# A decoder layer on one core: other phases for the stages of the feed-forward and cross-attention part, and x rounded two rows at a time

## The reference

```python
x = _layernorm(x + _L0_attn_ref(x, ...))        # gated linear attention, 16 heads
x = _layernorm(x + _L0_xattn_ref(x, ctx, Wq, bq, Wk, bk))
x = _layernorm(x + _L0_ffn_ref(x, w_gate, w_up, w_down))

def _L0_xattn_ref(x, ctx, Wq, bq, Wk, bk):
    query, key = ctx @ Wq.T + bq, ctx @ Wk.T + bk           # 512 x 128 each
    return x @ softmax(query @ key.T)                       # over the feature axis of x

def _L0_ffn_ref(x, w_gate, w_up, w_down):                   # 2048 inner features
    gate, up = bitlinear(x, w_gate), bitlinear(x, w_up)
    return bitlinear(fwht(silu(gate) * up), w_down)

def bitlinear(x, w):       # per token: round(x * 128/absmax) in -128..127; w ternary
    return act_quant(x) @ weight_quant(w).T
```

## Time and profile before

| | |
|---|---|
| median of 3 runs | 1765.03 us (1763.45 to 1766.21) |
| the profiled execution | 1764.3 us, of which the span of the instructions is 1762.5 |
| granted TensorE clock, mean | 0.958 |
| busy: TensorE, VectorE, ScalarE, GpSimd | 1569.6, 1050.5, 678.7, 468.5 us |
| first gate, end of the span | 1264.4, 1762.5 us |

### The profile page before, as it was taken

How to read it: one execution, slowest core, us unless ns; L and a number is a source line. 1 busy time by engine, 2 the same in 40 slices (tenths; PEclk the granted TensorE clock), 3 DMA queues, 4 the chain that set the end, 5 groups by cost and what they waited for, 6 DMA issues and landing times. The chain is left out here.

```text
span 1762.5 us, 24103 instructions
## 1 busy us (share of the span) xinstructions
PE 1569.6 (89%) x9570; PEld 1233.5 (70%) x9570; DVE 1050.5 (60%) x1962; ACT 678.7 (39%) x1276; POOL 468.5 (27%) x334
## 2 busy tenths in 40 slices
PE   7999999999999999999999999987676868878765
PEld 5888777888788887888877878875453545655553
DVE  4555655556555566565565655667666667765544
ACT  4323323223233233332332323322356566576632
POOL 1112001012001113333443333310255543344300
PEclk9999999999999999999999999998888989999887
DMA  7011101101111001211111111021011332323430
GB/s 252 31 49 37 49 30 53 32 31 59 38 36 55 25 13 48 67 36 61 60 44 65 54 50 57 27 94 74 13 42 56 100 96 66 92 76 108 127 106 18
DMA packets 86527, 107.00 MB, mean 61 GB/s; under 512 B 4496, under 2 KB 58896, under 8 KB 86032
## 3 DMA queue, kind: packets, MB, share of 16 engines
q1 hardware_dynamic: 84496, 99.17, 17.5%
q0 software_dynamic: 1920, 6.29, 0.9%
HBM read 78.19 MB, written 27.26 MB: 60 GB/s over the span
## 5 line engine op out<-in xcount | busy, mean ns | idle before, releaser
L350 PE MATMUL bank<-Wh,XTh 128*128 128x512 f32 x512 | 211.5, 413 | 0.0
L352 PE MATMUL bank<-Wh,XTl 128*128 128x512 f32 x512 | 200.8, 392 | 0.0
L351 PE MATMUL bank<-Wl,XTh 128*128 128x512 f32 x512 | 199.9, 390 | 0.0
L682 ACT ACTIVATE V<-bank 128x256 f32<-128x256 f32 x128 | 49.1, 384 | 373.2 <-PE bank L352 373.1
L1257 POOL TENSOR_TENSOR sm<-sm,half 128x8 f32<-128x8 f32 x32 | 52.8, 1649 | 522.9 <-DVE sm L973 522.9
L350 PE MATMUL bank<-XTh,Wh 128*128 128x512 f32 x384 | 160.9, 419 | 12.1 <-DVE XTl L868 12.1
L352 PE MATMUL bank<-XTh,Wl 128*128 128x512 f32 x384 | 151.0, 393 | 0.0
L351 PE MATMUL bank<-XTl,Wh 128*128 128x512 f32 x384 | 150.2, 391 | 0.0
L908 DVE SCALAR_TENSOR_TENSOR U<-U,bank 128x256 f32<-128x256 f32 x128 | 53.6, 419 | 148.3 <-ACT U L684 148.3
L563 PE MATMUL bank<-XT,W 128*128 128x512 bf16 x512 | 125.8, 390 | 11.9 <-ACT H L808 7.0
L1292 POOL TENSOR_TENSOR M<-GS,M 128x512 f32<-128x512 f32 x64 | 81.9, 1280 | 182.3 <-ACT GS L796 168.8
(11 more groups left out here) (188 smaller groups left out, 3423.9 us busy)
## 6 DMA issues: line engine op xcount, KB each, us to landing
z_scratch<-EV SPq DMA_DIRECT2D x64, 256.0 KB, 2.0
Z<-z_scratch SPq DMA_DIRECT2D x16, 1024.0 KB, 5.8
RAW<-wgT SPq DMA_DIRECT2D x16, 512.0 KB, 3.8
RAW<-wuT SPq DMA_DIRECT2D x16, 512.0 KB, 3.7
RAW<-wdT SPq DMA_DIRECT2D x16, 512.0 KB, 3.7
w_scratch<-BW POOLq DMA_DIRECT2D x24, 256.0 KB, 4.3
W<-w_scratch SPq DMA_DIRECT2D x3, 2048.0 KB, 14.0
RAW<-Wo SPq DMA_DIRECT2D x8, 512.0 KB, 3.8
```

Source lines behind the costliest of these rows:

```text
L350: engine.matmul(o, lh(c), rh(c), start=c == 0, stop=False)
L351: engine.matmul(o, lh(c), rl(c), start=False, stop=False)
L352: last = engine.matmul(o, ll(c), rh(c), start=False, stop=c == n - 1)
L682: engine.activation(V[:, par, i, :], bk[:, 0:256], ACT.Copy).then_inc(S["v_evac"], 1)
```

## The change

In the feed-forward list, `clamp` of tile i goes from step 4i+27 to 4i+29, `turn_q` from 4i+28 to 4i+31, `down` from 4i+29 to 4i+32 and `store` from 4i+30 to 4i+33; `quantise` stays at 4i+26. The list is three steps longer. The cross stages get a table of their own places (`BESIDE`): `qk` goes from the last step of a block into the first one of the next, behind its gate; the four normalisations of n1 become a stage; `x101` and `x123` join `energy23` and `att_scale`; `x_turned` goes from the 14th to the 16th step of a block. In the seam `n1` stands behind `energy23`, and `leave_o` ahead of `xm3`. `x_round` is now two stages of two rows each, with the small scale operations twice, for two rows each time.

```diff
+CROSS = ("ctx", "qk", "n1", "energy01", "energy23", "att_scale", "att01", "att23", "x101", "x123", "xm0", "xm1",
+         "xm2", "xm3", "x_round0", "x_round1", "x_made", "x_turned")
+
+BESIDE = {0: ("qk",), 1: ("n1",), 2: ("energy01",), 3: ("energy23", "x101"), 4: ("att_scale", "x123"),
+          5: ("att01",), 6: ("att23",), 8: ("xm0",), 9: ("xm1",), 10: ("xm2",), 11: ("xm3", "x_round0"), 12: ("x_round1",),
+          13: ("x_made",), 15: ("x_turned",)}
...
-        if n % 4 == 3 and 0 <= (n - 27) // 4 < 16:
-            yield "clamp", (n - 27) // 4
+        if n % 4 == 1 and 0 <= (n - 29) // 4 < 16:
+            yield "clamp", (n - 29) // 4
...
-        if n < 46:
-            yield CROSS[(n + 2) % 16], (n + 2) // 16 + 1
-        if n % 4 == 0 and 0 <= (n - 28) // 4 < 16:
-            yield "turn_q", (n - 28) // 4
-        if n % 4 == 1 and 0 <= (n - 29) // 4 < 16:
-            yield "down", (n - 29) // 4
+        if b < 3:
+            for stage in BESIDE.get(j, ()):
+                yield stage, b + 1
+        if b < 2 and j == 14:
+            yield "ctx", b + 2
+        if n % 4 == 3 and 0 <= (n - 31) // 4 < 16:
+            yield "turn_q", (n - 31) // 4
+        if n % 4 == 0 and 0 <= (n - 32) // 4 < 16:
+            yield "down", (n - 32) // 4
...
-                elif stage == "x_round":
-                    act.wait_ge(S["x_scale"], b + 1)
+                elif stage in ("x_round0", "x_round1"):
+                    k = int(stage[7])
+                    act.wait_ge(S["x_scale"], 2 * b + k + 1)
...
-                    for i in range(4):
+                    for i in (2 * k, 2 * k + 1):
...
+                elif stage == "n1":
+                    for i in range(4):
+                        normalise("n1", 4 * b + i, i)
```

More of the change, by code:

```diff
@@ L74, in seam_order @@
     return (("keys", last), ("ctx", 0), ("scores", last), ("states", last), ("turn_o", last - 1), ("qk", 0),
-            ("ok", last), ("y", last - 1), ("turn_ok", last), ("energy01", 0), ("energy23", 0), ("turn_w", last), ("att01", 0),
+            ("ok", last), ("y", last - 1), ("turn_ok", last), ("energy01", 0), ("energy23", 0), ("n1", 0), ("turn_w", last), ("att01", 0),
             ("weights", last), ("att23", 0), ("x101", 0), ("x123", 0), ("values", last), ("xm0", 0), ("xm1", 0),
-            ("turn_o", last), ("xm2", 0), ("xm3", 0), ("leave_o", 0), ("x_round", 0), ("y", last), ("leave_y", 0),
+            ("turn_o", last), ("xm2", 0), ("leave_o", 0), ("xm3", 0), ("x_round0", 0),
+            ("x_round1", 0), ("y", last), ("leave_y", 0),
             ("x_made", 0), ("x_turned", 0))
-CROSS = ("ctx", "qk", "energy01", "energy23", "att_scale", "att01", "att23", "x101", "x123", "xm0", "xm1", "xm2",
-         "xm3", "x_round", "x_made", "x_turned")
+CROSS = ("ctx", "qk", "n1", "energy01", "energy23", "att_scale", "att01", "att23", "x101", "x123", "xm0", "xm1",
[3 more added lines that the diff above has]
+          13: ("x_made",), 15: ("x_turned",)}
 def ffn_order():
-    yield CROSS[0], 1
-    yield CROSS[1], 1
-    for n in range(64 + 27):
+    yield "ctx", 1
+    for n in range(64 + 30):
+        b, j = divmod(n, 16)
         if 0 <= n - 22 < 64:
@@ L98, in ffn_order @@
             yield "read", (n - 18) // 4
-        if n % 4 == 3 and 0 <= (n - 27) // 4 < 16:
-            yield "clamp", (n - 27) // 4
+        if n % 4 == 1 and 0 <= (n - 29) // 4 < 16:
+            yield "clamp", (n - 29) // 4
         if n % 4 == 2 and 0 <= (n - 26) // 4 < 16:
             yield "quantise", (n - 26) // 4
-        if n < 46:
-            yield CROSS[(n + 2) % 16], (n + 2) // 16 + 1
-        if n % 4 == 0 and 0 <= (n - 28) // 4 < 16:
-            yield "turn_q", (n - 28) // 4
-        if n % 4 == 1 and 0 <= (n - 29) // 4 < 16:
-            yield "down", (n - 29) // 4
-        if n % 4 == 2 and 0 <= (n - 30) // 4 < 16:
-            yield "store", (n - 30) // 4
+        if b < 3:
[7 more added lines that the diff above has]
+            yield "down", (n - 32) // 4
+        if n % 4 == 1 and 0 <= (n - 33) // 4 < 16:
+            yield "store", (n - 33) // 4
 def raw_tasks():
@@ L547, in cross @@
                     bk = take(("spread", b), (S["s_evac"], b + 1))
-                    pe.wait_ge(S["x_scaled"], b + 1)
+                    pe.wait_ge(S["x_scaled"], 4 * b + 4)
                     for i in range(4):
@@ L1053, in cross @@
                     row_max(b, 1)
-                    normalise("n1", 4 * b, 0)
-                    normalise("n1", 4 * b + 1, 1)
                 elif stage == "energy23":
@@ L1094, in cross @@
                     dve.wait_ge(S["y_mm"], 4 * STEPS)
[L1095 to L1098, removed]
+                elif stage in ("x_round0", "x_round1"):
+                    k = int(stage[7])
+                    q = ax[:, b, :, 2 * k:2 * k + 2]
+                    if k:
+                        finish(b, 3)
+                    dve.wait_ge(S["x_absmax"], 4 * b + 2 * k + 2)
                     engine.tensor_scalar(q[:, 0, :], q[:, 0, :], EPS, 1.0 / 128, ALU.max,
                                          ALU.mult).then_inc(S["x_limit"], 1)
-                    dve.wait_ge(S["x_limit"], b + 1)
+                    dve.wait_ge(S["x_limit"], 2 * b + k + 1)
                     engine.reciprocal(q[:, 1, :], q[:, 0, :]).then_inc(S["x_scale"], 1)
@@ L1106, in cross @@
                     engine.tensor_scalar(q[:, 3, :], q[:, 0, :], ws[:, 1, 0:1], float(1.0 / np.sqrt(np.float32(FF))),
-                                         ALU.mult, ALU.mult)
+                                         ALU.mult, ALU.mult).then_inc(S["x_scaled"], 1)
                 elif stage == "x_made":
@@ L1140, in ffn_tile @@
                     dve.wait_ge(S["h_scale"], 4 * i + 1)
+                    dve.wait_ge(S["x_scaled"], 4 * b + 4)
                     engine.tensor_scalar(f[:, 6:7], f[:, 4:5], ax[:, b, 3, i % 4:i % 4 + 1], EPS, ALU.mult,
```

## The result

The changed kernel takes 1772.01 us (median of 5 runs, 1771.09 to 1772.50); the kernel before took 1763.45 us beside it (5 runs, 1762.53 to 1766.21). The ratio is 1.0044, 95% interval 1.0029 to 1.0059: slower, by 8.6 us between the medians, where 1756 was forecast. The profiled execution took 1771.41 us, its span is 1769.6, 7.1 more than before.

A forecast was written before the change was run, and what follows sets the result against it. The prediction took a ScalarE-VectorE ring to pace the feed-forward steps, with TensorE's wait for the clamp mostly lead. Its terms, -13.7-1.3+4.5-2.8+5.0 = -8.3 us on 1764.3, gave 1756; own range 1748 to 1763, with rivals 1739 to 1773.

The forecast's parts named there:

- the sum: Whole kernel: -13.7-1.3+4.5-2.8+5.0 = -8.3 us on the profiled 1764.3, giving 1756.0.
- Start and block 0: Feed-forward start to tanh 16: gate 0 and tanh 0 fit under the first wait, tanh 16 at 1344.8, -13.7 us.
- Block 1: Tanh 16 to tanh 32: steps sum to 102.0 us against 103.3 before, -1.3.
- Block 2: Tanh 32 to tanh 48: stages paired otherwise, the merged step dear; 116.2 us against 111.7 before, +4.5.
- Block 3: Tanh 48 to tanh 63, without cross stages: 80.9 us, -2.8.
- the ring: Feed-forward steps: ScalarE and VectorE alternate, each starting when the other ends, 4.48 us from eviction to eviction in a late step.
- The wait for the clamp: TensorE's 42.4 us ahead of turn_q: mostly lead over ScalarE and VectorE, so it goes with blocks 2 and 3 hardly shorter.
- The rival that TensorE's waits pace the kernel: Feed-forward part: removing TensorE's waits gains about 37 us, 1728, or 1742 with the tail alone TensorE-bound; chance 0.15.
- The tail: Tanh 63 to the end: 14.1 us per tile against 15.1, but one tile more behind the last gate; 110.3 us, +5.0.
- its sign of being wrong: The forecast would be wrong if block 2 fell below 105 us or the tail's interval left 13.5 to 15.
- the rival: Behind the last gate: each down at the lower clock, 6.2 us, interval 16.4, tail 125.1, total 1771; chance 0.25.

The follow-up runs named there:

- cross part alone: The change with the feed-forward tile stages (clamp, turn_q, down, store) back at their old places: 1753.19 us, ratio 0.9929.
- tile part alone: The kernel before with only clamp, turn_q, down and store at the places of the change: 1784.13 us, ratio 1.0104.
- long filler: The change with 22 useless matmuls into an unread bank ahead of each down from tile 8 on: 1761.62 us, ratio 0.9992.
- short filler: The change with eight useless matmuls into an unread bank ahead of each down from tile 8 on: 1770.86 us, ratio 1.0029.
- late `down`: The change's cross-attention places with clamp and turn_q at old places, down and store two steps later than in the kernel before: 1711.62 us, ratio 0.9707.

## Why the prediction was wrong

The sign was wrong by one term, the duration of `down` behind the last gate. The profiled execution is 15.4 us above the sum: 10.6 are the tail's, 4.8 the blocks'. Without the tail's the change would have been 3.5 us faster. By the prediction's own steps:

**Start and block 0: right, and 3.3 us too modest.** Gate 0 and tanh 0 went into the wait for the low half (tanh 0 at 1256.83). Tanh 1 was put at 1269.6 and came at 1266.2, because `qk` did not take the 5.3 us of the earlier trace rows:

```profile
1258.19 0.50 PE L358 MATMUL bank<-X1h,XH 128*128 128x512 f32 x1 [2.12 <-POOL X1l L1275]
...
1260.83 0.39 PE L360 MATMUL bank<-X1h,XL 128*128 128x512 f32 x1
1261.06 1.25 PE L571 MATMUL bank<-XT,W 128*128 128x512 bf16 x5
```

TensorE idles 2.12 us instead of 5.83 ahead of it, since gate 0 is its filler, and it does `qk` in 3.0 us: the clock over `qk` is 1.00, and was 0.50 before. The forecast had kept the slow clock for `qk` although it had put work in front of it: the error of the tail with the other sign. From tanh 1 to 16 were 75.3 us, forecast 75.2.

**Block 1: right.** 100.7 against 102.0.

**Block 2: the sign right, the size too small.** 120.1 against 116.2. The cross part alone has 116.4 there, the tile part alone 113.7, before 111.7: +4.7 and +2.0, and some 1.7 more together. The cross part is the dear one, as forecast. By steps the miss sits in 43 to 45, with `x_round0`, `x_round1` and `x_made`: put at 19.7 together, they took 23.9, and 22.3 in the cross part alone. The slow `down` in step 44 (5.20 us) is not it: with the long filler that `down` took 3.61 and the step 7.8 all the same. The step with the four normalisations was put at 7.3 and took 7.4; here they are, and below them those of block 0:

```profile
1452.96 3.85 DVE L1018 TENSOR_SCALAR Y<-Y,mv,rs 128x512 f32<-128x512 f32 x4
```

```profile
1266.05 1.91 DVE L1018 TENSOR_SCALAR Y<-Y,mv,rs 128x512 f32<-128x512 f32 x4
```

In block 0 GpSimd does nothing from 1265.36 to 1267.63, nearly to their end, and the four take 1.91 us (block 1 the same); in block 2 GpSimd's product begins at 1453.34, among them, and they take 3.85. The Trainium skill, "SBUF — State Buffer", section "SBUF: two separate sides", states that a VectorE operation in a two-port mode and a GpSimd one each hold the pair of ports which they share for the whole instruction. The trace agrees. The forecast had 2.0 for the four without a collision and 3.3 with one.

**Block 3: the sign wrong.** 86.4 against 80.9. In the timeline of TensorE, two downs that stand in the same place of their cycle:

```profile
1583.18 3.61 PE L604 MATMUL bank<-W,HT 128*128 128x512 bf16 x16 [2.52 <-ACT HT L830]
...
1604.84 5.30 PE L604 MATMUL bank<-W,HT 128*128 128x512 bf16 x16 [2.52 <-ACT HT L830]
```

The step with the first is 5.0 us from tanh to tanh, the one with the second 6.7: the gate behind `down` comes late to the ring. Two of the block's four downs took 5.3 us, so this is 3.4 us of the miss of 5.5; 1.0 is the first cycle (23.4 against 22.4), the rest is spread. Which of these downs is slow is partly luck: up to tile 8 both filler runs have the list of the change, and there steps 52, 56 and 60 have one slow `down` (long filler) and three (short filler) instead of two. Each makes its step 6.5 to 6.7 us instead of 5.0, and block 3 takes 85.1, 86.4 and 88.7 us with one, two and three. These steps are also where the late `down` is better: its block 3 is 81.4 and all its downs there take 3.6. So the same term failed here already, as a smaller sum.

**The wait for the clamp: right.** 35.1 of the 42.4 us of TensorE's waiting went, and the blocks were not shorter for it: the tile part alone, which takes that wait away too, reached the last tanh 2.7 us later than before. The rival that TensorE's waits pace the kernel, 1728 or 1742, is refuted: cross stages and the start account for the gain at tanh 63. Most of that wait had lain behind the last gate in any case: inside the blocks the trace of before has

```profile
PE bank L589 <- DVE HQ L1156: 9.4, 4, 2.9
```

and that smaller number is the one that should have stood in the argument.

**The tail: this step failed.** The serial part was put at 10.2 us, and is 10.4 in five intervals (1708.22, where a down ends, to 1718.64, where the next begins) and 8.5 in the last: 60.6 in the six, 0.6 less than forecast. The first down was to end 8.8 behind tanh 63, the six intervals to take 84.6, the last tile 11.3 and the end 5.6. Measured are 9.9, 95.5, 10.0 and 5.6. The intervals carry +10.9 of +10.6. In them `down` was priced at 3.5 to 4.3 from the earlier trace rows, 23.4 in all, and took 4.9 to 6.5, 34.9 in all: +11.5, the whole miss and a little more. A mean interval of 15.9 is outside the 13.5 to 15 that the prediction had named as its sign of being wrong. The downs of the earlier trace rows are of a kernel in which `turn_q` (1705.10, 1.87 us) and a product of `had2` run directly ahead of the `down` at 1708.57; the change puts 5 us of idle time there, while the copies of `turn_q`'s output stand behind the next rounding. I had named that in the rival, with the row that shows its price, 6.20 us for a `down` at the lower clock, and it came out at 1771 where 1772 was measured. Its mechanism is right, that it hit to 1 us is luck: it had tanh 63 at 1644 and a tail of 125.1, measured are 1648.6 and 120.9, and the two misses cancel. It had 0.25 and should have had most of the weight: the sum itself let `down` wait for the copies HT until 10.2, behind a rounding of 2.4 us, with little for TensorE to do meanwhile, and the rows of before in which `down` follows idle time gave a warning: the last one with 6.20, and one in block 3 with 5.21 us behind 2.31 of idle time. The long filler shows that with the clock the intervals of the sum are right: six of them 84.3 against 84.6; its tail is 112.0 against 110.3.

**What the change lost.** Three more places between rounding and transposes gave nothing in the tail, because there the rounding of tile i+1 and the copy HT of tile i meet in the same two queues, and `down` waits for both. A place is only distance if no longer stage stands in it in the queue of the engine that makes the input. The place that was missing was between `turn_q` and `down`, where `had2` of the next tile keeps TensorE going.

What stays open: what each place of the new cross part is worth beside the late `down`, beyond the three steps named above; and why of two downs in the same place of their cycle one is fast and the other slow.

## What to carry to other kernels

Before a group of matmuls is priced from a row, look at how long TensorE idles ahead of that row and ahead of the group in the new order, and take the row that is alike: here the same sixteen matmuls were 3.6 or 6.5 us, and that was the sign of the result. Where TensorE idles only for some 2.5 us the same order gave both prices, so carry the two as a range. When a stage is moved away from what it waits for, count the distance in the queue of the engine that makes its input, not in steps of the list, and put TensorE's ready work directly ahead of the group that must be fast. A wait of TensorE that is only lead over a ring of other engines can go without a gain.

## What the hardware showed that I had not expected

- Eight matmuls of filler (1.67 us) with 3.35 us of idle time behind them left `down` at 6.57 us; 22 (4.91 us) with 0.34 behind them brought it to 3.61. More work on TensorE made the whole kernel 9 us faster.
- Equal idle time directly ahead is not enough to tell the clock: the two downs of block 3 above both follow 2.52 us of it, and took 3.61 and 5.30. Nor is the same order of work: at the same place of the list a `down` was fast in one execution and slow in the next, and a step of block 1 took 5.0 us at a clock of 1.00 and 7.6 at 0.74. A difference of 2 or 3 us between two single profiles can be that.
- The sixteen transposes of `turn_q` took 1.87 us in the tail before, 1.13 with the late `down`; the clock over them was 0.50 and 1.00. The slow clock had been in that tail too, so even the kernel before paid for it.
